# Ten products without use on TensorE in the last step of each attention layer, gate weights loaded in steps 11 to 18, and logits, sums and statistics at other places

## What is computed

```python
def attn_a(x):                       # 16 heads of 8 features
    q, k, v = proj(x, wq, bq), proj(x, wk, bk), proj(x, wv, bv)
    scores = einsum('bhqd,bhkd->bhqk', q, k) / sqrt(8)
    attn = softmax(scores + causal_mask)
    return einsum('bhqk,bhkd->bhqd', attn, v) @ wo + bo

def attn_b(x):                       # 16 heads of 8 features, no mask
    q, k, v = x @ W_qkv + b_qkv
    sim = -(q_row_2 - 2.0 * q @ k.T + k_col_2) / (fro_q * inf_xt)
    return softmax(sim) @ v @ W_proj + b_proj

def ffn(x):                          # 8 experts of 128 -> 512 -> 128
    rw, idx = softmax(top_2(x @ Wr))
    h = silu(x @ Wg[e]) * (x @ Wu[e])
    return sum(rw_e * (h @ Wd[e]) * 12 ** -0.5 for e in idx)

x = x + attn_a(layernorm(x)); x = x + ffn(layernorm(x))
x = x + attn_b(layernorm(x)); x = x + ffn(layernorm(x))
```

## Time and profile before

| | before |
|---|---|
| three runs, median (fastest to slowest) | 1102.22 us (1089.67 to 1113.69) |
| the profiled execution | 1107.71 us, its span 1105.3 us |
| mean granted clock of TensorE | 0.933 |
| TensorE busy | 993.8 us, 90% |
| VectorE busy | 771.1 us, 70% |
| ScalarE busy | 712.6 us, 64% |
| GpSimd busy | 542.9 us, 49% |
| attention A, steps 4 to 19 | from 61.5 to 329.1 us |
| expert loop 0 | from 330.5 to 547 us |
| attention B, steps 2 to 19 | from 548.0 to 878.1 us |
| expert loop 1 and the last gathers | from 879 us to the end |

### The profile page before, as it was taken

One profiled execution on the slowest core, in us unless ns is written; L12 is line 12 of the kernel. 1 busy time (PEld: TensorE's weight loads), 2 busy tenths in 40 slices (PEclk: granted clock), 3 DMA queues, 4 the chain that ended last, 5 costly groups with the idle time before them and its releaser, 6 DMA issues.

```text
span 1105.3 us, 28185 instructions
## 1 busy us (share of the span) xinstructions
PE 993.8 (90%) x9148; PEld 701.1 (63%) x9148; DVE 771.1 (70%) x2335; ACT 712.6 (64%) x1399; POOL 542.9 (49%) x764
## 2 busy tenths in 40 slices
PE   2999999998988999998889899999988799999992
PEld 1345545554458999998734344445643589999992
DVE  4688878878677534465789989998687774443554
ACT  2367767765554566666558779999667555666661
POOL 3144445644650630255787846588416416204655
PEclk9999989999888999999959889999787799999996
DMA  5545766643223765675644434344321246667774
GB/s 154 115 109 126 178 163 140 163 109 95 61 69 90 185 168 146 159 185 149 173 102 110 108 91 89 90 100 97 70 61 45 77 112 176 158 148 170 190 189 140
DMA packets 239303, 139.86 MB, mean 127 GB/s; under 512 B 92724, under 2 KB 215352, under 8 KB 239160
## 3 DMA queue, kind: packets, MB, share of 16 engines
q1 hardware_dynamic: 230968, 121.29, 45.1%
q0 software_dynamic: 8192, 16.79, 5.2%
HBM read 87.86 MB, written 50.14 MB: 125 GB/s over the span
## 4 chain that ended last, share of the span: by engine, by line
PE 31%; DVE 10%; issue 4%; DMA 3%; SPq 3%; POOL 1%; ACT 1%; POOLq 0%; DVEq 0%; ACTq 0%
PE psS L364 5%; PE psO L330 4%; PE psT L1422 4%; PE psS L1415 4%; DVE mx L670 4%; PE psO L1436 2%; PE psN L1436 2%; PE psN L337 2%; DMA wuc<-in_L_ffn_Wu 1%; PE psM L285 1%; SPq L1509 1%; DMA xin<-xg 1%; DVE row L610 1%; PE psM L435 1%; PE psM L294 1%
## 5 line engine op out<-in xcount | busy, mean ns | idle before, releaser
L670 DVE TENSOR_REDUCE mx<-psS 128x3 f32<-128x384 f32 (+1 forms) x512 | 310.2, 618 | 94.2 <-PE psS L395 53.6
L364 PE MATMUL psS<-kst,qst 48*128 48x256 bf16 (+1 forms) x1024 | 196.4, 280 | 39.4 <-DVE mx L670 28.4
L567 ACT ACTIVATE pT<-psT,scb 128x512 f32<-128x512 f32 x256 | 193.3, 772 | 48.4 <-PE psT L372 45.5
L372 PE MATMUL psT<-qst,kst 50*128 50x256 bf16 (+1 forms) x1024 | 191.5, 274 | 7.2 <-DMA qst<-scr_m 4.8
L1298 POOL DMA_INDIRECT xg<-xn,slot x128 | 123.2, 962 | 127.5 <-DVE ysb L1483 75.0
L1462 ACT ACTIVATE sg<-psS 128x512 f32<-128x512 f32 x142 | 84.8, 597 | 145.3 <-PE psS L1415 142.7
L1422 PE MATMUL psT<-xTt,wuc 128*128 128x128 f32 x1136 | 155.1, 280 | 4.9 <-DMA wuc<-in_L_ffn_Wu 4.6
L562 ACT ACTIVATE pT<-psT 128x384 f32<-128x384 f32 x256 | 123.5, 488 | 55.1 <-PE psT L372 47.2
L1415 PE MATMUL psS<-xTt,wgc 128*128 128x128 f32 x1136 | 153.7, 279 | 4.2 <-DVE xTt L1475 4.2
L364 PEld LDWEIGHTS psS<-kst,qst 48*128 48x128 bf16 x1024 | 63.2, 96 | 139.0 <-DVE mx L670 72.3
L1488 DVE TENSOR_TENSOR hT<-sg,psT 128x512 f32<-128x512 f32 x142 | 97.0, 683 | 71.6 <-PE psT L1422 52.7
(11 more groups left out here) (228 smaller groups left out, 1621.4 us busy)
## 6 DMA issues: line engine op xcount, KB each, us to landing
wuc<-in_L_ffn_Wu SPq DMA_DIRECT2D x142, 256.0 KB
scr_part<-part SPq DMA_DIRECT2D x128, 128.0 KB, 2.4
qst<-scr_part SPq DMA_DIRECT2D x64, 192.0 KB, 3.6
kst<-scr_part SPq DMA_DIRECT2D x64, 192.0 KB, 4.6
eo<-ysb SPq DMA_DIRECT2D x142, 64.0 KB
xin<-xg SPq DMA_DIRECT2D x280, 32.0 KB
scr_part<-part SPq DMA_DIRECT2D x32, 192.0 KB, 2.1
xg<-zero SPq DMA_DIRECT2D x7, 576.0 KB, 3.7
```

The source lines that it names most:

```text
L364: return nc.tensor.matmul(ps[:, c0:c0 + n], q_[r64, t, q0], k_[r64, t, 0:n], start=(half == 0), stop=True, skip_group_check=True)
L372: return nc.tensor.matmul(ps[:, c0:c0 + T - q0], k_[m64, t, half * P:half * P + P], q_[m64, t, q0:T], start=(half == 0 or not L.causal), s ...
L567: nc.scalar.activation(pT[:, g % 8, 0:cols], psT[g % 2][:, 0:cols], ACT.Exp, scale=scb[r][:, 0, i:i + 1], bias=scb[r][:, 1, i:i + 1]).then ...
L670: nc.vector.tensor_reduce(mx3[:, u, 0:n, pos:pos + 1].rearrange("p a b -> p (a b)"), psS[h % 2][:, 0:kcols(L)].rearrange("p (a k) -> p a k ...
```

## The change

- **TensorE, step 19 of both attention layers.** Ten matrix products (`pe_warm`) of the bf16 identity with 512 columns of `kst[0]` are added: four behind head 12, three behind head 13, three behind head 15. They write into `psS[0]`, and nothing reads them.
- **SP, attention A.** The gate weights are loaded in steps 11 to 18 instead of 4 to 11, at the same point of the step. The down weights are loaded in steps 3 to 10 instead of 4 to 11.
- **TensorE, step 15 of attention B.** The four groups of logits, four products each, stood at heads 3 to 6. Now two products stand at each of heads 3 to 10. VectorE's copy of them moves from head 8 to head 11.
- **VectorE, attention B.** In step 6 the second four adds stand at head 5 instead of head 7, as in the other steps. The four statistics that stood at head 5 of step 6 stand at head 9 of step 5.
- **VectorE, expert loops.** The sums of blocks 4 to 15 start at `at` = 11, 15 and 19 instead of 13, 18 and 23. In loop 0 the layer norm of these blocks starts at 23 instead of 27, and GpSimd's gathers of the first half come two a tile instead of three in two tiles.

```diff
-        def pe_logits(pe, n, i):
+        def pe_logits(pe, n, i, half=None):
...
-            for m in range(4):
+            for m in range(4) if half is None else range(2 * half, 2 * half + 2):
...
-            last.then_inc(r["lg_ps"], 1)
+            if half is None or half:
+                last.then_inc(r["lg_ps"], 1)
...
-                pool.wait_ge(f_sem["y"], n0 + OWN + (2 * pair // 3 if l == 0 else pair // 2) + 1)
+                pool.wait_ge(f_sem["y"], n0 + OWN + pair // 2 + 1)
...
-            if 4 <= j < 4 + E and point == 3:
-                e = j - 4
+            if 3 <= j < 3 + E and point == 3:
+                e = j - 3
                 sp.dma_start(wd[:, e * HID:(e + 1) * HID].rearrange("p (k d) -> p k d", k=HB),
                              A["L0_ffn_Wd"][e].rearrange("(k p) d -> p k d", p=P)).then_inc(s_wffn, 16)
-            if 4 <= j < 4 + E and point == 1:
-                e = j - 4
+            if 11 <= j < 11 + E and point == 1:
+                e = j - 11
                 sp.dma_start(wg[:, e * HID:(e + 1) * HID], A["L0_ffn_Wg"][e]).then_inc(s_wg, 16)
...
+        WARM_AT = {12: 4, 13: 3, 15: 3}
+
+        def pe_warm(count):
+
+            for _ in range(count):
+                nc.tensor.matmul(psS[0][:], identb[:], kst[0][:, 0:2, :].rearrange("p t q -> p (t q)"), start=True, stop=True, skip_group_check=True)
...
-                    if 3 <= h < 7:
-                        pe_logits(pe, n, h - 3)
+                    if 3 <= h < 11:
+                        pe_logits(pe, n, (h - 3) // 2, h % 2 == 0)
...
+                if j == 19 and h in WARM_AT:
+                    pe_warm(WARM_AT[h])
...
-            if (j, h) == (6, 5):
+            if (j, h) == (5, 9):
                 dve.wait_ge(r_sem["x"], 2 * mid)
                 link(dve_stats(lo + 4, mid))
...
-            if (j, h) == (15, 8):
+            if (j, h) == (15, 11):
                 dve_logits(dve, n, 0, QUADS[0], LG_COPIES[n] + 1)
...
-                if l == 1 and j in SUMS_AT and h in (3, 7 if j == 6 else 5):
+                if l == 1 and j in SUMS_AT and h in (3, 5):
                     dve_combine_half(dve, 0, SUMS_AT.index(j), int(h > 3))
...
-            for q, first in ((1, 13), (2, 18), (3, 23)):
+            for q, first in ((1, 11), (2, 15), (3, 19)):
                 if first <= at < first + 4:
                     dve_combine_0(dve, l, 4 * q + at - first)
...
-                if at == 27:
+                if at == 23:
                     dve.wait_ge(r_sem["x"], 2 * HALF)
-                if 27 <= at < 32:
-                    for h in (2 * (at - 27), 2 * (at - 27) + 1):
+                if 23 <= at < 28:
+                    for h in (2 * (at - 23), 2 * (at - 23) + 1):
                         dve_ln_at(dve, h, 4, HALF - 4, s_lnB, 2)
```

## The result

The changed kernel takes 1086.78 us in the median of 20 runs (1077.55 to 1095.26), the kernel before 1102.97 us in the median of 20 (1089.67 to 1113.69). The ratio is 0.9886, with a 95% interval of 0.9858 to 0.9915: 0.9 to 1.4% faster. The means of all these runs are 16.5 us apart (13.4 to 19.9). The forecast was 1091.0 within 1079 to 1106. Single runs of the changed kernel spread over 18 us and of the kernel before over 24, so each difference comes with a 95% interval from resampling, and each is against the runs of before of the same session unless it is said otherwise.

What follows compares the result with a forecast made beforehand. TensorE, busy for 90% of the span, loses time where it waits or its clock is low; 5.0 + 5.5 + 4.0 + 1.0 + 1.2 = 16.7 us off the profiled 1107.7 gives 1091.0 us, range 1079 to 1106.

Steps and rivals of the forecast that it cites:

- Part 1, the loads: Attention A: with the gate loads moved, the row maxima's trip through DRAM is no longer late; 5.0 us gained.
- The term of 5.8 us for steps 9 and 10: Attention A: TensorE's 1.8 us wait on the row maxima and the clock fall behind it go; 5.8 us gained.
- The 2.0 us that I held back for new stalls in steps 12 and 13: Attention A: the moved gate loads newly stand ahead of the maxima's trip in these two steps; 2.0 us lost.
- The trip takes about 1.4 us in steps 4 to 10: Attention A, sign of being right: the row maxima go to DRAM and back in about 1.4 us.
- Part 2, the sums: Attention B, step 6: adds at head 5 shrink, TensorE's 3.25 us wait and the clock fall go; 5.5 us gained.
- Part 3, the logits: Attention B, step 15: two products a head let scores stand between and the clock holds; 4.0 us gained.
- Part 4, the products: Step 19, both layers: ten added products let the first gate group run at full clock; 1.0 us gained together.
- Part 5, the loops: End of loop 0: the layer norm chain moves from ahead of the last copies, shortening TensorE's waits; 1.2 us gained.
- The clock falls anyway: Rival, attention layers: clock falls stay and mostly only waits go; 5.9 us gained, 1101.8 us; chance 25%.
- The loads stall steps 12 and 13: Rival, attention A: the queue keeps its order and both steps pay 5.8 us; 1100.6 us; chance 12%.
- More falls go: Rival: earlier ends shift what follows and further clock falls vanish; about 8 us more, 1083 us; chance 15%.
- VectorE becomes the bound of the loops: Rival, expert loops: sums in 12 tiles in a row leave VectorE no catch-up; 22 us, 1113 us; chance 6%.

Runs made afterwards that it cites:

- alone: The kernel before with one part's edit only, mean us: moved loads 1096.6, sums and statistics 1098.7, logits 1097.9, ten products 1101.3, expert loops 1098.8.
- in company: The changed kernel with one part put back as before, mean us: old loads 1094.3, no ten products 1089.0, old loops 1088.8.
- The late sums: The kernel before with the second four adds at head 7 in steps 3, 4, 6 and 7 of attention B: mean 1116.1 us, 14.5 slower.

## Why the prediction held, step by step

The time came out 4 us under the forecast and inside the range, and faster, as forecast. Those 4 us are the start of the sum: I took 16.7 us off the profiled execution's 1107.7, while the 20 runs of before have a median of 1103.0. The sum itself was 16.7 us; the runs give 16.5 for the whole, the five parts alone 16.7 together, and the stage means of the parts 13.5 (5.8 + 4.9 + 3.6 - 0.7 - 0.1), so that 3 us have no place in the table. That the sum is met this closely is in part luck: several terms were wrong and cancel, and each part alone is known to 3 us or so at best.

- **Part 1, the loads: 5.0 forecast, 5.4 alone and 7.6 in company.** Right in sum, wrong in its terms. The term of 5.8 us for steps 9 and 10 came from one execution, and that one was the worst of six: without the moved loads these steps took 32.6 to 36.7 us, 34.3 on average, and the gain is 2.5. The 2.0 us that I held back for new stalls in steps 12 and 13 weren't lost: these two took 36.5 us with the loads there and 36.2 without. And steps 4 to 8 and 14 to 16, for which I had 1.2 us, gave 2.7, neither difference clear of noise; in 14 to 16 TensorE waits for no maxima with or without the loads, so what was gained there isn't known. "The trip takes about 1.4 us in steps 4 to 10" was wrong: it takes 2.5 us in step 9 and 2.3 in step 10, with no gate load ahead of it; it is early enough all the same.
- **Part 2, the sums: 5.5 forecast, 3.4 alone, 4.9 in the stages.** Right in the mechanism, with adds of 1.93 us as in step 4. I had taken step 4 as the model for step 6 (18.4 us), but it became like step 7 (19.90 at clock 0.91), which was the lower bound. The wait doesn't tell the two apart: in steps 4, 6 and 7 alike TensorE waits 1.55 us for VectorE behind the adds, and in step 4 the clock stays at 1.00. The late sums showed the mechanism at three more places.
- **Part 3, the logits: 4.0 forecast, 4.2 alone, 3.6 in the stages.** Right by two errors that cancel. The stretch of the earlier trace rows takes 18.57 us at full clock, not 21.4. I had added the 3.8 us of products to a whole step 14. But the stretch is a head short of a step, and step 14 holds eight transposes of tokens that step 15 hasn't, in two groups like this one:

```profile
749.15 0.60 PE L992 MATMUL psO<-ident,xn 128*128 128x128 f32 x4
```

From second residual to second residual, where the steps are whole, step 14 takes 17.5 us and step 15 takes 20.2, so that 2.7 of the 3.8 us are to be seen; TensorE is idle for only 0.4 us of step 14, so idle time hides next to nothing. The gain at full clock was thus larger than my 4.7. Against it, 1.7 us came back behind it on average, which I hadn't charged, 0.8 of it in two profiles of seven and 0.9 in one.

- **Part 4, the products: 1.0 forecast, 0.8 alone, 2.3 in company, -0.7 in the stages.** Not to be told from zero. The step that TensorE would stop next at VectorE's layer norm was right, and the row shows it (2.73 us ahead of L992). What I missed is that the clock falls behind that stop. The delay of the last residual, the cost I had bounded by 0.7 us a layer, was 0.4 us in attention A of the changed kernel (5.58 us between the two residuals of step 19, where the profiles of the table without products have 5.19 to 5.29), but over the five profiles with ten products it is 0.2 to 2.0 us (5.43 to 7.18), beyond the bound in two. The second projection, whose lateness I had named as a sign of being wrong, does come later in the changed kernel: 5.0 us behind the first residual of step 19 for 4.3 in attention A, 5.7 for 5.0 in attention B.
- **Part 5, the loops: 1.2 forecast, 2.9 alone, 2.1 in company, -0.1 in the stages.** Not to be told from zero. The step that failed is that the chain alone held the last copies. With it gone TensorE waits 0.98 and 1.24 us, against 0.97 and 1.66: 0.4 us, and in the profile of the edit alone even more than before. The next late thing is the store of `eo`, which I hadn't looked for.
- **The rivals.** "The clock falls anyway" (5.9 us) fell: the gain is 16.5 us, and the clock's part shrank by 16. Its waits did go, though: without the ten products the other part is 5.0 us lower than before. "The loads stall steps 12 and 13" fell: in step 12 the write follows 3.9 us behind the load and the trip takes 1.3 us, in step 13 it follows 3.1 us behind and takes 2.5, and TensorE waits for neither. "More falls go" may have been partly so, in steps 4 to 8 and 14 to 16 of attention A (not clear of noise), and was partly the reverse, in step 15 of attention B in two profiles. "VectorE becomes the bound of the loops" fell: VectorE's waits on token loads are 61.9 us where they were 72.9, so the slack is still there.

## What to carry to other kernels

In a kernel whose TensorE is busy for 90% and runs at two clock levels, a wait can cost more than itself, by a stretch at the lower level around it: here 7.2 us of added waits cost 14.5. It need not: the same wait of 1.55 us had such a stretch with it in step 7 and none in step 4. Size such a place from several executions: the profiled execution of before took 5 us more than the median of its kernel, and the step that looked worst in it was worst partly by chance. Work without use that keeps the clock up gained nothing here that is clear of noise, since another engine stopped TensorE soon behind it and the fall came there.

## What the runs showed of the hardware

VectorE's adds and GpSimd's split took turns to the point that four adds of 1.12 us in all took 3.83; I had known of the 3.66 us in one step, not that it comes back at every place where the two meet. The same work behind the same TensorE waits (step 18 of attention B) ran with 17.1 us at the lower clock in one profile and with none in another. And span times clock differs between runs of one kernel by less than the time does: over the 87 runs of before its standard deviation is 3.0 us, that of the time 5.6 and that of the clock's part 6.8. The time goes with the clock's part (correlation 0.89) and hardly with the other (-0.17), so it is in the stretches at the lower level that two runs of this kernel differ; what makes them differ there stays open.
